# Attention heads: the order of row-score halves, maxima, outputs and transposes on TensorE

## What is computed

```python
q_hyp, k_hyp = exp_map0(q_tan, curv), exp_map0(k_tan, curv)
q_time = sqrt(1.0 / curv + sum(q_hyp * q_hyp, -1))      # k_time likewise
attn_logits = -(q_hyp @ k_hyp.T - q_time * k_time.T) / sqrt(HD)
attn = softmax(attn_logits, axis=-1)
out = attn @ v_tan
x = layernorm(h + out @ wo_w.T + wo_b)
```

## Time and profile before

| | us |
|---|---|
| median of 3 runs | 6156.74 |
| lowest, highest | 6152.11, 6157.6 |
| span of the profiled execution | 6144.5 |

### The profile page before, as it was taken

How to read it: one execution, slowest core, us unless ns; L and a number is a source line. 1 busy time by engine, 2 the same in 40 slices (tenths; PEclk the granted TensorE clock), 3 DMA queues, 4 the chain that set the end, 5 groups by cost and what they waited for, 6 DMA issues and landing times. The chain is left out here.

```text
span 6144.5 us, 94514 instructions
## 1 busy us (share of the span) xinstructions
PE 5024.7 (82%) x27420; PEld 2060.5 (34%) x27420; DVE 4853.2 (79%) x10599; ACT 3730.4 (61%) x5393; POOL 1063.6 (17%) x1465
## 2 busy tenths in 40 slices
PE   6979899797979989795999754427888888887878
PEld 3333333333333333332666522211111111115555
DVE  6767675776767576775888678888999999997878
ACT  5555555555565555553444367767888888885534
POOL 0001000000000000000111100003444444444521
PEclk8989999898999989897999976655555555558999
DMA  0000000000000000000111123332111111115522
GB/s 25 1 8 8 8 8 1 15 1 13 4 8 8 1 15 1 8 1 30 39 41 41 48 92 128 128 129 66 48 52 48 51 48 52 49 46 176 177 87 72
DMA packets 198911, 273.67 MB, mean 45 GB/s; under 512 B 13989, under 2 KB 157989, under 8 KB 192454
## 3 DMA queue, kind: packets, MB, share of 16 engines
q1 hardware_dynamic: 181190, 252.90, 13.2%
q10 hardware_dynamic: 17408, 16.78, 0.8%
HBM read 151.14 MB, written 118.49 MB: 44 GB/s over the span
## 5 line engine op out<-in xcount | busy, mean ns | idle before, releaser
L663 DVE TENSOR_REDUCE at_nmax<-at_ps_t 128x1 f32<-128x512 f32 x2048 | 1318.9, 686 | 480.9 <-PE at_ps_t L344 459.8
L498 ACT ACTIVATE at_probsT<-at_ps_s 128x1024 f32<-128x1024 f32 x1024 | 992.3, 1021 | 799.0 <-PE at_ps_s L375 799.0
L2075 DVE SCALAR_TENSOR_TENSOR sc_decayed<-sc_da,sc_state 128x256 f32<-128x256 f32 x2048 | 771.4, 420 | 8.5 <-ACT sc_da L2030 8.5
L344 PE MATMUL at_ps_t<-at_qkT 108*128 108x512 bf16 x2048 | 734.7, 407 | 50.2 <-DVE at_nmax L663 18.9
L2037 ACT ACTIVATE sc_xd<-sc_ps_du,sc_bt 128x512 f32<-128x512 f32 x1024 | 650.0, 692 | 176.8 <-PE sc_ps_du L1978 176.8
L2085 DVE CUSTOM_DVE_ANT_0 sc_state<-sc_xd,sc_decayed 128x256 f32<-128x256 f32 x2048 | 749.3, 402 | 1.3 <-DVE sc_decayed L2075 1.3
L1943 POOL TENSOR_SCALAR sc_xd<-sc_xd 128x1024 f32<-128x1024 f32 x512 | 532.2, 1040 | 805.1 <-ACT sc_xd L2037 805.1
L1967 PE MATMUL sc_da<-sc_parts,sc_sel 24*128 24x512 bf16 x1024 | 568.1, 609 | 119.6 <-DMA sc_sel<-sc_sel 83.9
L1978 PE MATMUL sc_ps_du<-sc_parts,sc_sel 24*128 24x512 bf16 x1024 | 565.2, 609 | 111.7 <-ACT sc_xd L2037 111.6
L366 PE MATMUL at_ps_s<-at_qkT 108*128 108x512 bf16 x2048 | 576.1, 386 | 17.1 <-ACT at_probsT L498 16.3
L2030 ACT ACTIVATE sc_da<-sc_da,sc_a_col 128x1024 f32<-128x1024 f32 x512 | 563.3, 1100 | 0.4 <-PE sc_da L1967 0.4
(11 more groups left out here) (307 smaller groups left out, 7518.8 us busy)
## 6 DMA issues: line engine op xcount, KB each, us to landing
dt_parts<-si_pt SPq DMA_DIRECT2D x64, 384.0 KB, 2.6
du_parts<-si_pu SPq DMA_DIRECT2D x64, 384.0 KB, 3.2
sc_parts<-dt_parts SPq DMA_DIRECT2D x128, 192.0 KB
sc_parts<-du_parts SPq DMA_DIRECT2D x128, 192.0 KB
u_tok<-si_ut SPq DMA_DIRECT2D x8, 2048.0 KB, 8.3
y<-sc_yo SPq DMA_DIRECT2D x256, 64.0 KB
so_yin<-y SPq DMA_DIRECT2D x32, 512.0 KB
so_uin<-u_tok SPq DMA_DIRECT2D x32, 512.0 KB
```

The source lines that it names most:

```text
L344: nc.tensor.matmul(ps_t[c][:], qkT[0:KP, hd, t * P:(t + 1) * P], qkT[0:KP, H + hd, c * HALF:(c + 1) * HALF], start=True, stop=True).then_i ...
L498: nc.scalar.activation(probsT[:, c % RING, :], ps_s[c % 2][:], ACT.Exp).then_inc(s_exp, 1)
L663: nc.vector.tensor_reduce(nmax[:, par, c, t:t + 1], ps_t[c][:], AX_X, ALU.max, negate=True).then_inc(s_max, 1)
L2075: nc.vector.scalar_tensor_tensor(decayed[:, ch], da[q % 2][:, j % 2, ch], DECAY_MIN, state[:, (j - 1) % SRING, ch], ALU.max, ALU.mult).the ...
```

## The change

On TensorE the order within a pair becomes: turned scores of tile c, half 0 of row scores c + 12, turned scores of tile c + 1, half 1 of row scores c + 12, the four maxima, half 0 of row scores c + 13, the sixteen output matmuls, half 1 of row scores c + 13. The maxima of both tiles are now issued by one call in the same order as before. `turned_back` goes from the middle of the pair c = 2 to the front of the pair c = 4, and on VectorE `inverses` and `weighted` go from after the reductions of c = 2 and c = 3 to after those of c = 4 and c = 5. `row_turned` stays where it is, and so do its two waits.

```diff
-            def row_scores(b, hd, t, first=False):
-                for c in range(2):
+            def row_scores(b, hd, t, halves=(0, 1), first=False):
+                for c in halves:
...
-                for u, bank in enumerate(logit_banks(c)):
-                    row = slice(u * VW, (u + 1) * VW)
-                    nc.tensor.matmul(bank, ones[row, :], nrows[row, par, :], start=False, stop=True
-                                     ).then_inc(s_logit, 1)
+                for n in (c, c + 1):
+                    for u, bank in enumerate(logit_banks(n)):
+                        row = slice(u * VW, (u + 1) * VW)
+                        nc.tensor.matmul(bank, ones[row, :], nrows[row, par, :], start=False, stop=True
+                                         ).then_inc(s_logit, 1)
...
-            def row_scores_ahead(b, hd, c, left):
+            def row_scores_ahead(b, hd, c, left, half):
                 ahead, t = (c + LEAD) // TB, (c + LEAD) % TB
                 if ahead <= left:
-                    row_scores(b, hd + ahead, t)
+                    row_scores(b, hd + ahead, t, (half,))
 
             def head(b, hd, par, left, first=False):
                 for c in range(0, TB, 2):
+                    if c == 4 and not first:
+                        turned_back(b, hd - 1)
                     if c == 6 and left:
                         row_turned(b, hd + 1, 1 - par)
-                    row_scores_ahead(b, hd, c, left)
-                    for n in (c, c + 1):
-                        turned_scores(b, hd, n, first and c == 0)
-                    if c == 2 and not first:
-                        turned_back(b, hd - 1)
-                    row_scores_ahead(b, hd, c + 1, left)
-                    for n in (c, c + 1):
-                        maxima_subtracted(b, hd, par, n)
+                    turned_scores(b, hd, c, first and c == 0)
+                    row_scores_ahead(b, hd, c, left, 0)
+                    turned_scores(b, hd, c + 1, first and c == 0)
+                    row_scores_ahead(b, hd, c, left, 1)
+                    maxima_subtracted(b, hd, par, c)
+                    row_scores_ahead(b, hd, c + 1, left, 0)
                     for n in (c - 2, c - 1):
                         if c > 0:
                             outputs(b, hd, n)
                         elif not first:
                             outputs(b, hd - 1, TB + n)
+                    row_scores_ahead(b, hd, c + 1, left, 1)
...
-                    if c == 2 and not first:
+                    if c == 4 and not first:
                         inverses(b, hd - 1)
-                    if c == 3 and not first:
+                    if c == 5 and not first:
                         weighted(b, hd - 1)
```

More of the change, by code:

```diff
@@ L418, in head @@
                             outputs(b, hd - 1, TB + n)
+                    row_scores_ahead(b, hd, c + 1, left, 1)
             def heads(b):
                 for n in range(LEAD):
-                    row_scores(b, n // TB, n % TB, n == 0)
+                    row_scores(b, n // TB, n % TB, first=n == 0)
                     if n == LEAD - 1:
```

## The result

The changed kernel takes 6213.0 us (median of 4 runs, 6206.2 to 6217.6) against 6155.8 us before in the same comparison. The ratio is 1.0094, 95% interval 1.008 to 1.0108: **0.9% slower, 57 us**. The forecast was 6218, +61. The profiled execution has a span of 6215.6 us, 71.1 more than that of before; it is one of the longer runs. In every run on record the time is 1.8 us above the span (here 6217.4 against 6215.6), so the 12.2 us between span and median of the kernel before are not what lies around a span: its profiled execution was a short one, by about 10 us. Of the 71 us between the two traces, 14 are thus a matter of which executions were profiled.

The account below looks back on a forecast made before the run. TensorE's own order was taken as the bound. Per head, 0.54 us gained and 1.18 lost gave 0.64 more, +67 us over 104 heads; with +1 and -7 that made +61, so 6218 us, range 6155 to 6295.

Parts of the forecast that it names:

- The bound: TensorE's own order bounds the kernel; two loops catch it now and then, about 1.0 us of each head waiting.
- part 1: Halves of row scores put one by one: four pairs and transposes take 14.41 us a head, 0.54 less than 14.95.
- The walked pair: One pair of TensorE's new order, followed step by step from its first turned score to the next pair: 3.49 us.
- The unseen change: TensorE's switch from full array to 32-column outputs, shown by no row: taken at 0.33 us, bounds 0.22 and 0.49.
- Part 2: Transposes and multiply moved back: row_turned waits 1.18 to 1.24 us behind pair 4 for the multiply, in 104 of 128 heads.
- The sum: Whole kernel: +67 us for 104 heads, +1 for the first sequence, -7 for heads 0 and 14, together +61 us.
- Head 14: In each sequence, gains in its two pairs with row scores and hides turned_back in a wait: together 0.4 us less.
- Head 0: First head of each sequence: gains in its three later pairs, about 0.4 us less.
- That the wait is hidden: Rival: row_turned's wait in pair 6 costs nothing, a head takes 14.41 us, time 6095 us; chance 0.08.
- Half hidden: Rival: pairs 6 and 0 have unseen room that covers half of row_turned's wait, 6157 us, no change; chance 0.08.
- row scores that still wait: Rival: row scores wait for reductions as before, about 0.7 us a head, time 6293 us; chance 0.05.
- The clock: Rival: the clock falls to 1.2 GHz for one pair per head with the longer wait, 6509 us; chance 0.03.

Follow-up runs that it names:

- the moves alone: Kernel before, old order of halves, with only turned_back moved to the front of pair 4 and inverses and weighted behind c = 4 and c = 5: 6175.9 us.
- the early multiply: Changed kernel with weighted on VectorE following the reductions of c = 4 instead of c = 5: 6090.9 us, ratio 0.9897 to the kernel before.
- its variant: Kernel with the early multiply, with the first pair of each sequence's head 0 issued as in the kernel before: 6090.8 us, ratio 0.99.

## Why the prediction was right

**The bound and part 1.** Right, step by step. The walked pair was 3.49 us, measured 3.48. The unseen change, from full array to column groups, was taken at 0.33 from its nearest rows and is 0.32 (511.66 to 511.98). No reduction and no exponential is waited for in it. A head without the new wait was worked out at 14.41 us; it measured 14.44 with transposes and multiply where they were, and 14.35 with the transposes where the change put them and the multiply early. Of the Trainium skill's rule on tiling modes (page "TensorEngine Tiling (Array Packing)", "Key Properties") this trace now shows all four kinds of change in a pair, each at 0.09 to 0.10 us beyond a matmul's 0.216; had the fourth been free, pairs would have taken 3.38.

**Part 2.** Right in mechanism, place, size and count. The wait was forecast at 1.18 to 1.24 us, with 1.18 in the sum, and is 1.23 (1.46 less 0.23); the transposes were to start 4.67 to 4.73 after the first turned score of pair 4 and start 4.71 after it (513.43 to 518.14); in 104 heads, as counted. One number in it was off and hidden by another: from the end of the multiply to TensorE there are 0.15 us, not the 0.06 taken from a half that waits for a reduction, and the multiply started only 0.61 behind the reduction's start, so that it ended at 4.56 in the pair's time (513.43 to 517.99), 0.05 ahead of the earliest end forecast.

**The sum.** Heads 1 to 13 were forecast at 15.59 and take 15.59: +69 us between the two traces. That it fits to 0.01 us is luck: without the wait a head takes 14.35 and not 14.41, and the wait adds 1.24 and not 1.18. Head 14 was to gain 0.4 us and gains 0.66 (the stretch from its transposes back to those of head 13: 14.28 before, 13.62 after), 5 us in all. Head 0 is the term that failed: it was to gain 0.4 us a sequence, 3 in all, and between the traces it lost 6. Its pairs were priced at the upper clock level, but TensorE comes into head 0 at the lower one: the clock rose 3.9 to 8.3 us into the stretch before, and 7.4 to 11.8 after. Here is one stretch of each, before and after, in which it rose at 8.3:

```profile
1516.30:1530.04 13.74, 13.60 (x74) 3.96 (x73) 8.76 (x15) 6.84 (x8) 3.22 (x6) 0.70 0.00 1
```

```profile
1195.58:1209.09 13.51, 13.51 (x74) 4.17 (x73) 8.46 (x14) 7.37 (x8) 1.60 (x6) 0.69 0.00 1
```

With the same rise the new order is 0.23 us shorter; the later rises cost more than that. That the change itself made them later is not shown: the kernel with the moves alone, with the old head 0, lost 4 us there against the same trace of before.

The terms give +70, the spans differ by 71. Two things outside the sum nearly cancel: between the sequences (from the last of these transposes in one to the first of the next) 3.4 us went, and behind the last of them 4.6 came. The unchanged part of that, from the last `turned_back` to the end, is 3334.5 us in the trace of before and 3339.6 to 3341.4 in all the others; the trace of before is, as said above, a short one. The median of the runs moved by 57 us, 4 less than forecast; with 14 us between this and the two spans, that it came so near is partly luck.

**The rivals.** That the wait is hidden needed the multiply ahead of the reduction; the experiment with the early multiply made exactly that, and the time fell to 6091, where this rival stood at 6095. TensorE started nothing past the waiting transposes, as the Trainium skill has it ("TensorE: Matmul & The Clock Gate", "The mechanism"). Half hidden, and row scores that still wait: neither is seen. The clock did not fall in the stretches with the longer wait: 1.00 over the head shown, and no time at the lower level between the transposes of head 0 and those of head 14 in any sequence.

## What to carry to other kernels

When work is moved later on one engine, look up every wait on its result and ask what will stand right ahead of the waiter and right ahead of the moved work: here one move put a half-tile at the end of a pair on TensorE, right ahead of the waiting transposes, the other put a multiply behind that half-tile's reduction, and the wait that they make together (122 us, by the run without it) is in neither alone (56 us faster and 23 us slower). The mend was one line, and with it the kernel takes 6090.9 us, 1% less than the kernel before. And work that stands in a wait is free only there: before moving it, price it as if it were new, and before counting a new wait, look for what will fall into it.

## What was not expected

Head 0 takes between 11.5 and 15.4 us in the eight sequences of one execution (the early multiply, repeated), by where in it the granted clock rises from 1.2 to 2.4 GHz; 13.08 us at 0.82 and 15.55 at 0.62 are shown above for its variant. A few such heads are as much as the changed kernel's runs differ by, 11 us. And a wait whose release is seen 0.06 us later at one instruction took 0.15 at another: between a multiply on VectorE and transposes on TensorE that wait for two semaphores.
